# Batch 29 gets places of its own, and the routing pieces, last chains, gathers and first 24 tiles are put in another order

## The reference

```python
x   = x + LN(MHA(q=LN(x), k=ctx, v=ctx) + LN(x)) * gamma + beta   # 32 batches, 100 queries, 361 keys, 16 heads of 16
y   = LN(x)                                                       # input of the second block
z   = LN(y) * ln_g + ln_b
p   = softmax(z @ rW + rb)                                        # 8 experts
w   = top2(p) / sum(top2(p))
h   = gelu(z @ W1[e] + b1[e])                                     # 256 -> 512
mix = sum over the two experts of w[e] * (h @ W2[e] + b2[e])      # 512 -> 256
out = x + y + mix
```

## Time and profile before

| | us |
|---|---|
| median of 3 runs | 885.03 (884.59 to 885.10) |
| the profiled execution | 884.46 |
| its span in the trace | 882.6 |
| attention at full rate, 50 to 560 of the span | PE busy 481.4 of 510 |
| routing, last chains and first tiles, 560 to 724 | PE busy about three quarters |
| tiles, 724 to 853 | PE busy nearly throughout |
| final add, from 853 on | one transfer |

### The profile page before, as it was taken

The page is one execution under the profiler, slowest core; times in us unless marked ns, Lnnn a source line. Parts: engine busy times, 40 slices in busy tenths (PEclk is TensorE's granted clock), DMA queues, the critical chain, the costliest instruction groups (busy, mean ns, idle before and its releaser), DMA issues.

```text
span 882.6 us, 26129 instructions
## 1 busy us (share of the span) xinstructions
PE 756.5 (86%) x8056; PEld 588.5 (67%) x8057; DVE 669.1 (76%) x1855; ACT 535.9 (61%) x1412; POOL 554.4 (63%) x609
## 2 busy tenths in 40 slices
PE   3669799999999999999999987557797889999970
PEld 1446477777777777777777665436686779998960
DVE  5279799999999999999999978883477745555540
ACT  3336488788888888878888864425353345555530
POOL 4133587786877777777777864343764566777840
PEclk9689899999999999999999999757899899999995
DMA  5674366767677586766767679512332344333337
GB/s 151 142 180 108 95 139 153 172 149 182 151 164 170 142 184 140 182 150 166 166 148 181 162 215 250 140 26 50 58 56 42 49 61 73 59 62 61 65 36 149
DMA packets 155690, 110.95 MB, mean 126 GB/s; under 512 B 68376, under 2 KB 149572, under 8 KB 155108
## 3 DMA queue, kind: packets, MB, share of 16 engines
q1 hardware_dynamic: 132598, 77.01, 38.2%
q0 software_dynamic: 11360, 17.37, 11.9%
q10 hardware_dynamic: 11678, 15.90, 6.2%
HBM read 39.90 MB, written 23.88 MB: 72 GB/s over the span
## 4 chain that ended last, share of the span: by engine, by line
PE 63%; DVE 13%; issue 7%; DMA 4%; DVEq 4%; POOL 3%; SPq 2%; ACT 1%; ACTq 1%; POOLq 0%
PE pj L864 10%; PE pj L833 9%; PE s_row L878 9%; PE zt L909 8%; PE s_t L897 8%; PE s_row L968 6%; PE pj L851 3%; PE pj L979 3%; DVE negmax L1338 3%; PE zt L979 2%; DVE v_neg L1440 1%; DMA zscr<-zn 1%; DVEq L1427 1%; DVEq L1435 1%; DMA z_in<-zscr 1%
## 5 line engine op out<-in xcount | busy, mean ns | idle before, releaser
L1338 DVE TENSOR_REDUCE negmax<-s_row 100x1 f32<-100x361 f32 x512 | 251.2, 523 | 24.7 <-PE s_row L878 17.5
L1161 ACT ACTIVATE p_t<-s_t 128x400 f32<-128x400 f32 x384 | 188.8, 501 | 66.6 <-PE s_t L897 60.0
L878 PE MATMUL s_row<-stack_x,q_stack 125*128 125x361 bf16 x512 | 133.1, 322 | 20.3 <-DVE negmax L1338 10.6
L897 PE MATMUL s_t<-q_stack,stack_x 128*128 128x100 bf16 x1536 | 128.8, 211 | 14.1 <-ACT p_t L1161 9.8
L897 PEld LDWEIGHTS s_t<-q_stack,stack_x 128*128 128x128 bf16 x1536 | 93.4, 99 | 60.4 <-issue 26.9
L968 PE MATMUL s_row<-w_qkv,v_aug 128*128 128x128 f32 x912 | 117.4, 284 | 13.6 <-DVE v_aug L1429 13.6
L968 PEld LDWEIGHTS s_row<-w_qkv,v_aug 128*128 128x128 f32 x912 | 111.4, 199 | 16.5 <-DVE v_aug L1429 14.7
L864 PE MATMUL pj<-w_qkv,ct 128*128 128x256 f32 x384 | 108.4, 406 | 0.0
L833 PE MATMUL pj<-ct,w_qkv 128*128 128x361 f32 x256 | 96.1, 500 | 10.2 <-DMA bk_s<-in_bk 9.1
L1147 ACT ACTIVATE w_qkv<-s_row,b_k 128x128 f32<-128x128 f32 x228 | 65.2, 369 | 61.7 <-PE s_row L968 61.6
L1343 DVE TENSOR_SCALAR p_t<-p_t 128x1200 f32<-128x1200 f32 x128 | 99.6, 778 | 0.1
(11 more groups left out here) (233 smaller groups left out, 1466.7 us busy)
## 6 DMA issues: line engine op xcount, KB each, us to landing
stack_x<-k_part SPq DMA_DIRECT2D x192, 192.0 KB, 3.9
q_stack<-q_part SPq DMA_DIRECT2D x186, 64.0 KB, 2.0
ct<-in_ctx_t SPq DMA_DIRECT2D x32, 361.0 KB, 5.0
stack_x<-in_w ACTq DMA_DIRECT2D x8, 512.0 KB, 6.4
w_s<-in_w ACTq DMA_DIRECT2D x14, 256.0 KB, 3.0
zscr<-zn SPq DMA_DIRECT2D x32, 100.0 KB
z_in<-zscr SPq DMA_DIRECT2D x32, 100.0 KB
zf_d<-zf_s SPq DMA_DIRECT2D x32, 100.0 KB
```

What stands on the lines that cost most here:

```text
L878: nc.tensor.matmul(s_row[h % 2][:, 0:KEYS], q_stack[0:MROW, b.slot, h, :], k_stack[0:MROW, b.slot, h, 0:KEYS], start=True, stop=True).then ...
L897: last = nc.tensor.matmul(s_t[g % 2][:, j * Q:j * Q + Q], k_stack[:, b.slot, h, kt * 128:kt * 128 + 128], q_stack[:, b.slot, h, 0:Q], star ...
L1161: nc.scalar.activation(p_t[:, quad % 2, kt, :], s_t[g % 2][:, 0:4 * Q], ACT.Exp).then_inc(exp_done, 1)
L1338: v.tensor_reduce(negmax[:, b.slot, h:h + 1], s_row[h % 2][0:Q, 0:KEYS], AXIS.X, ALU.max, negate=True).then_inc(max_done, 1)
```

## The change

Only tables change. `TAIL_FROM` goes from 30 to 29, `TAIL` becomes one table for each of the batches 29, 30 and 31, `due`, `span_of` and `occupant_before` look up the table of the batch. No instruction is added or removed; nearly all of `ROUTE_PLACE` and all of `TILE_PLACE` get new numbers.

```diff
-TAIL_FROM = B - 2
+TAIL_FROM = B - 3
-    for span, table in (("middle", PLACE), ("tail", TAIL), ("start", START)):
+    for span, table in (("middle", PLACE), ("start", START), *TAIL.items()):
-        return "tail"
+        return n.index
-            place = TAIL["PE"].get(user, place)
+            place = TAIL[index]["PE"].get(user, place)
-ROUTE_PLACE = {"sum_const": 326, "ask0": 369, "exp0": 369, "prob0": 370, "choose00": 372, "choose01": 373, "sum0": 374,
-               "ends0": 376, "places0": 377, "taken0": 378, "split0": 379, "hot00": 379, "hot01": 379, "number00": 380, "number01": 380, "query00": 380, "query01": 380,
-               "lanes00": 381, "lanes01": 382, "lanes02": 383, "lanes03": 384, "gates0": 374, "store0": 376, "picks0": 386, "experts0": 386, "index0": 387,
-               "gather": 388, "rows": 391, "affine": 391, "tiles": 391, "gelu": 391,
-               "ask1": 404, "exp1": 405, "prob1": 406, "choose10": 407, "choose11": 409, "sum1": 411, "gates1": 411, "store1": 413, "ends1": 413, "places1": 414,
-               "taken1": 415, "split1": 416, "hot10": 417, "hot11": 418, "hot12": 419, "hot13": 420, "query10": 418, "query11": 419, "query12": 420, "query13": 421,
-               "lanes10": 421, "lanes11": 422, "experts1": 423, "picks1": 423, "index1": 425}
-TILE_PLACE = [393 + 2 * k for k in range(NF)]
+ROUTE_PLACE = {"sum_const": 327, "ask0": 368, "exp0": 370, "prob0": 369, "choose00": 374, "choose01": 374, "sum0": 374, "ends0": 377, "places0": 378,
+               "taken0": 379, "split0": 379, "hot00": 380, "hot01": 380, "number00": 381, "number01": 381, "query00": 379, "query01": 381, "lanes00": 381,
+               "lanes01": 382, "lanes02": 383, "lanes03": 384, "gates0": 374, "store0": 379, "picks0": 385, "experts0": 386, "index0": 386, "gather": 391,
+               "rows": 390, "affine": 391, "tiles": 389, "gelu": 392, "ask1": 403, "exp1": 403, "prob1": 407, "choose10": 407, "choose11": 408,
+               "sum1": 411, "gates1": 408, "store1": 414, "ends1": 412, "places1": 414, "taken1": 418, "split1": 418, "hot10": 419, "hot11": 419,
+               "hot12": 420, "hot13": 422, "query10": 418, "query11": 421, "query12": 422, "query13": 424, "lanes10": 423, "lanes11": 423, "experts1": 424,
+               "picks1": 425, "index1": 431}
+TILE_PLACE = [393, 393, 395, 396, 397, 400, 404, 407, 407, 409, 411, 413, 416, 416, 418, 419, 420, 421, 423, 427, 431, 431, 432, 434]
-TAIL = {"PE": {"z": 8, "zft": -6, "router": -5}, "ACT": {"td": 8, "u": 2, "y": 5, "zft": -6}, "DVE": {"z": 8, "stats": 0, "var": 1, "stats2": 3, "var2": 4, "logits": -5}, "POOL": {"u": -1, "rstd": 1, "xb": 0, "y": 2, "rstd2": 4}, "SP": {"zout": 8, "zin": 9, "zf": -7}}
+TAIL = {29: {'PE': {'z': 7, 'zft': 1, 'router': 2}, 'ACT': {'td': 5, 'u': 5, 'y': 13, 'zft': 1, 'zt': 5}, 'DVE': {'z': 8, 'stats': 2, 'var': 3, 'stats2': 7, 'var2': 10, 'logits': 4}, 'POOL': {'u': 0, 'rstd': 1, 'xb': 0, 'y': 9, 'rstd2': 9}, 'SP': {'zout': 4, 'zin': 8, 'zf': 1}},
+        30: {'PE': {'z': 8, 'zft': -9, 'router': -6}, 'ACT': {'td': 9, 'u': 2, 'y': 5, 'zft': -7, 'zt': 4}, 'DVE': {'z': 8, 'stats': 0, 'var': 1, 'stats2': 3, 'var2': 4, 'logits': -6}, 'POOL': {'u': -1, 'rstd': 0, 'xb': 3, 'y': 3, 'rstd2': 6}, 'SP': {'zout': 9, 'zin': 11, 'zf': -4}},
+        31: {'PE': {'z': 7, 'zft': -7, 'router': -6}, 'ACT': {'td': 8, 'u': 3, 'y': 5, 'zft': -6, 'zt': 5}, 'DVE': {'z': 8, 'stats': 0, 'var': 1, 'stats2': 3, 'var2': 4, 'logits': -6}, 'POOL': {'u': -1, 'rstd': 1, 'xb': -6, 'y': 4, 'rstd2': 4}, 'SP': {'zout': 6, 'zin': 11, 'zf': -11}}}
```

## The result

The changed kernel takes **878.57 us** (877.88 to 881.28, six runs), the kernel before on the same chip 884.92 (884.59 to 886.83): a ratio of 0.9931, 95% interval 0.9919 to 0.9943. It is faster by 6.3 us, half of the 12.4 that were forecast. The profiled execution took 878.16, its span 876.3.

What follows compares the result with a forecast made beforehand. PE bounds most of the kernel, with waits from 560 to 724; DVE rules steps 6 to 16. Step 6 gains 10.3 (start's 3.9 included), the spread 2.1: 12.4 off 884.46 is 872.1, plus 0.57 gives 872.6 us, range 868 to 879.

Steps and rivals of the forecast that it cites:

- The start: Up to tile step 0 on PE: gathers behind rstd2 of batch 30 let it begin at 604.0, not 607.87: 3.9 us.
- at about 593.2' as before: Batch 30's var2, ahead of the first gather: unchanged in time, 0.5 to 1 us lost upstream being given back.
- 0.73 and two small operations: POOL between var2 of batch 30 and the first gather: rstd2 done at 594.4, gather at 594.5.
- Steps 0 to 6: Batch 31 between the tiles: step 6 begins on PE at 629, not 639.95, 10.3 us with the start's 3.9 included.
- The rival that waits only move: Batch 31's y comes later by two steps, DVE's waits only move, step 6 at 638: 883 to 885, chance 0.09.
- the query's wait: Tile 16: ACT's query10 waits for DVE's hot10, PE idles up to 5 us, DVE covers it by 1.0.
- the size of the spread: Steps 6 to 21: group 1's pieces over fifteen steps instead of ten, DVE ruling throughout, gain 2.1 us.
- The rival of the uncovered wait: Steps 15 and 16: DVE stands with PE, up to the whole 5 us come on top: 877.6, chance 0.13.
- Behind it nothing changes: From PE's step 22, at 711.7 instead of 724.07, to the end: the 12.4 us gained stay.
- the rival of the slow clock: Steps 6 to 21: gaps keep PE at half clock, 31.5 us longer than forecast at fifteen slow steps: 904, chance 0.08.
- Both signs of being wrong: Named as wrong: DVE waiting for PE between 630 and 704, or a first gather after 597.
- The rival that batch 29's load lands late: Batch 29's u starts at 568 instead of 565, everything behind its stats 3 us late: 875.7, chance 0.13.

Runs made afterwards that it cites:

- e3: Changed kernel with picks0 moved on PE ahead of batch 29's transpose: 879.23 us, ratio 0.9926 to the kernel before.
- e2: Changed kernel with POOL's u of batch 30 moved ahead of rstd2 of batch 29: 879.48 us, ratio 0.9934 to the kernel before.
- e7: Changed kernel with ACT's copy of batch 30's values moved behind the exponential that DVE waits for: 878.62 us, ratio 0.9920 to the kernel before.
- e8: Changed kernel with the moves of e7, e2 and e3 together: 877.45 us, ratio 0.9908 to the kernel before.
- e10: Changed kernel with batches 29, 30 and group 0's pieces at old places, gathers behind rstd2, z of batch 31 one slot later: 879.15 us, ratio 0.9927.
- e5: Kernel before with only the first gathers moved on POOL, behind rstd2 of batch 30: 881.89 us, ratio 0.9960.
- e4: Changed kernel with query10 moved on ACT one slot later, behind the scaling of tile 16: 877.04 us, ratio 0.9922 to the kernel before.
- e11: e10 with query10 one slot later, behind the scaling of tile 16: 876.72 us, ratio 0.9902 to the kernel before.
- e12: Changed kernel with 14 unused identity matmuls added on PE in the wait for tile 24's gather: 878.83 us, ratio 0.9924 to the kernel before.
- the kernel with all three repairs: Changed kernel with the old start, query10 one slot later and 14 identity matmuls together: 874.88 us, ratio 0.9874 to the kernel before.
- e6: Changed kernel with group 1's pieces and tile steps from 6 on at the places of the kernel before: 878.60 us, ratio 0.9923.

## Why the prediction was half right

The sign, the order of events and the two large mechanisms were right; the size was twice what was measured. On PE the forecast had 604.0, 629 and 711.7 for steps 0, 6 and 22 and 12.4 at the end. Measured were 607.17, 632.48, 715.97 and 6.3. The missing 6.1 divide as follows.

- **The start, 3.2 of the 6.1, the step that failed.** Two terms were mis-sized. `var2` of batch 30 "at about 593.2' as before" came at 595.40: 2.2. I had counted 0.5 to 1 us lost upstream and given back, in one sentence and without following `u` of batch 30 on POOL. That `u` now stands behind `rstd2` of batch 29, an operation that used to run in a free moment and now lasts 2.58. DVE's statistics wait for `u`, and PE's `picks0` waits for the rows that come of `rstd2`; the chain that ended last goes through `picks0` in the changed kernel, and in `e3`, where `picks0` is ahead, through `u`. ACT's copy of batch 30's values holds up DVE's guard besides, so that no single repair helps (`e2`, `e3`, `e7`) and all of them together recover 1.7 at `var2` (`e8`), the old start the same (`e10`). By the means of the five traces with each start 1.8 is the order; the rest lies within what executions differ by. The second term: from `var2` to the first gather I took 1.3 us, "0.73 and two small operations", and it was 2.25 in `e5`, in `e10` and after alike. The `gain` operation alone takes 0.66 just ahead of a gather (0.19 on average in the kernel before), and the issue 0.45. From the gather to step 0 9.5 were forecast and 9.5 measured, in the other traces with the moved gathers 9.0 to 10.3, so the exact match is luck.
- **Steps 0 to 6, 0.3.** 25.0 forecast, 25.3 measured. DVE's wait for `y` ended at 628.31, with step 0 3.2 late and the rest of the chain as worked out. Six steps of 3.74 are 22.4; PE waited 1.49 and 0.52 us ahead of batch 31's transpose and router, and these two operations take most of the remaining 0.9. The rival that waits only move falls: the two long waits of DVE lost 5.9 us between them.
- **Steps 6 to 22, 0.8.** 82.7 forecast, 83.5 measured, and 82.5 with the query moved (`e4`, `e11`). So the stretch without the query's wait was sized rightly and the cover wrongly; the size of the spread alone the traces give no better than above. The query's wait was 4.60, up behind it ran slow, and DVE waited for PE at steps 16 and 17, 0.67 and 0.84, where 0.21 stands without a wait. The rival of the uncovered wait came true with 1 us of its 5. Up to step 16 the working holds: DVE's steps 14 and 15 took 9.9 us (673.25 to 683.15), 9.8 forecast, and the slow up left the cover short by some 0.5. What it left out is the step behind: DVE's step 16 has no piece beside it and took 3.6 with that wait (683.15 to 686.71), a step of PE takes 3.74, so DVE waited once more. Nor did DVE rule throughout: the chain that ended last runs mostly over PE from 651 to 668 and from 678 to 699.
- **Behind step 22, 1.8.** "Behind it nothing changes" failed. DVE, now the bound up to here, gives tile 20's result later against PE's own steps. From the result to step 22 it is the 6.5 of before, so the moment is right, but PE waits 3.90 us of it, not 2.92, and its clock falls. I had weighed the rival of the slow clock only for the steps 6 to 21, and as all or nothing. Of the 1.8, the matmuls gave 1.5 back in the trace (`e12`), and no trace with a fast up there shows more than 0.3 of the 1.8.

Both signs of being wrong that the forecast named came: the first gather after 597, and a DVE that waits for PE. The rival that batch 29's load lands late isn't what happened: POOL's `u` of 29 ran at 564.99, 565.24 before. In the forecast's list of losses the wait of 4.1 us for `picks1` is missing. Two slips in its rivals are of 0.1 and bear on nothing: 872.6 and 3 are 875.6, and 3.74 times 1.89 is 7.1. What of the start is due to the guard and what to `rstd2` of 29 stays open, and so does the sum in the time: by the intervals only the kernel with all three repairs stands well clear of the changed one.

## What to carry to other kernels

Where a change reorders several engines at once, the term "as before" is the one to work out step by step: follow each moved operation's successors on its own engine, above all the small ones of a slow engine that land beside a busy neighbour. A wait that a change makes longer has a second price, in the clock of the work behind it, so read the length of every wait that stays, not only of those that go. And an engine with three obstacles ahead of it is not freed by removing one.

## What the runs showed of the hardware

POOL's small operations stretch beside some work of DVE. `rstd2` on 100x2 takes 0.71 us at 595.62 and 2.58 at 584.44, and what DVE does at that time is (its timeline, changed kernel):

```profile
584.28 1.48 DVE L1391 TENSOR_TENSOR k_part<-stats,v_aug 100x1280 bf16<-100x1280 f32 x1
585.67 0.78 DVE L1343 TENSOR_SCALAR p_t<-p_t 128x1200 f32<-128x1200 f32 x1
586.37 1.49 DVE L1391 TENSOR_TENSOR k_part<-stats,v_aug 100x1280 bf16<-100x1280 f32 x1
```

In the kernel before it was `xb` that fell there, 1.97 instead of 0.73 at 590.55 of the changed kernel, and the same DVE operation beside it, which began while POOL's `u` was running, took longer too:

```profile
584.19 2.01 DVE L1391 TENSOR_TENSOR k_part<-stats,v_aug 100x1280 bf16<-100x1280 f32 x1
```

The page "SBUF — State Buffer" of the Trainium skill, section "Who interferes with whom", says that a DVE instruction with two SBUF inputs contends with a GpSimd one that reads SBUF; these rows agree. In `e10` DVE's operation of this kind had ended (585.15 and 1.48) when POOL's `xb` of batch 30 began, and it took its usual time (POOL, timeline of `e10`):

```profile
587.18 0.72 POOL L740 TENSOR_TENSOR xb<-stack_x,row_c 100x256 f32<-100x256 f32 x1
```

The sizes fit a wait that lasts to the end of the operation that began first: `xb` of the kernel before ends 0.6 us behind DVE's operation (586.79 and 586.20), about its usual 0.73. But in the changed kernel DVE's operation on `p_t` lies beside `rstd2` too, with one input only, and another `xb` took 1.14 at 594.12 beside such an operation (593.70, 0.98). No run was made to take one neighbour away, so which of them holds POOL up was read and not tested.

The length of a wait alone doesn't decide whether PE's clock falls. Ahead of step 22 waits of 2.92, 2.98 (`e5`) and 3.66 (`e11`) left up at 1.95 us, full speed, while waits of 2.95 (`e6`, up 3.62), 3.71 (`e4`, up 2.99) and 3.90 (up 3.40) were followed by a slow up, and so were the five of 3.87 to 4.03 in `e2`, `e3`, `e7`, `e8` and `e10`. What else decides was not found.
